# Reordering the front of a fused mLSTM and mixture-of-experts kernel: where statistics, square roots, queries and copies stand in each engine's queue

## The chip, the core and the metric

The kernel runs on one core of one Trainium2 chip. The metric is the device time of one execution in microseconds (us). All of the work is fp32 except for a few bf16 helper matrices.

## What is computed

The input is x, 16 sequences of 256 tokens with 128 features. It is normalised per token, an mLSTM attention and a top-1 mixture of experts both read the normalised xn, and the result is `x + s * silu(ffn)`:

```python
x = L0_attn_x                                  # 16 x 256 x 128
xn = _layernorm(x, axis=-1)
s = _L0_attn_ref(xn, wq, wk, wv, wi, bi, wf, bf, ln_w)
g = _silu(_L0_ffn_ref(xn, router_w, router_b, w1, b1, w2, b2))
x = x + s * g

# _L0_attn_ref, 4 heads of 32: q, k, v are 4x4 block-diagonal maps of xn
gate_in = jnp.concatenate([x, x, x], axis=-1)
ig = (gate_in @ wi.T + bi); fg = (gate_in @ wf.T + bf)
log_fg = jax.nn.log_sigmoid(fg)                # cumulated over the sequence: cs
log_D = where(tril, cs_i - cs_j, -inf) + ig_j
max_log_D = jnp.max(log_D, axis=-1, keepdims=True)
C = (q @ k.T / sqrt(dh)) * jnp.exp(log_D - max_log_D)
normaliser = jnp.maximum(abs(sum(C)), jnp.exp(-max_log_D))
h = C / (normaliser + eps) @ v                 # then a layernorm per head, times (1 + ln_w)

# _L0_ffn_ref, 8 experts: the expert with the largest router logit computes
a, g = jnp.split(x @ w1[i] + b1[i], 2, axis=-1)
y = (a * sigmoid(g)) @ w2[i] + b2[i]
```

## The kernel before

Nothing schedules this kernel: each engine has one program written out by hand, and semaphores join them. An engine goes through its queue in the written order, so an instruction that waits holds all that stand behind it on that engine. Engines: TensorE (PE), VectorE (DVE), ScalarE (ACT), GpSimd (POOL), and SyncE (SP), which issues most DMAs.

**Front.** The 32 tiles of 128 tokens form four groups of eight, g = 0 to 3. VectorE computes mean and variance of a group in `variance(g)` (`bn_stats` L696, `bn_aggr` L699, then `veps` L701, which raises `s_var`). ScalarE takes the square root in `rsqrt_start(g)` (L483, waits for `s_var` at g + 1, raises `s_y0`). VectorE turns it into 1/sqrt by a reciprocal and one Newton step in `newton(g)` (L707 to L711, waits for `s_y0`, raises `s_rsq`). In `normalised(g)` the eight tiles are then normalised, shared by VectorE (L716), ScalarE (L488) and GpSimd (L399). TensorE transposes them four at a time (`transposes(q)`, q = 0 to 7, L1037), ScalarE copies each four to SBUF (`xT_copy(q)`, L493), and TensorE multiplies them with the value, router and gate weights (`values(q)`, L1052), whose results `evac_vl(c)`, c = 0 to 10, takes out of PSUM: on VectorE for c = 1, 3, 5, 7, 9 (L723), on ScalarE for the others (L499). The small weights are first combined on TensorE (L1062 to L1065; their block matrices come from GpSimd, L392) and copied by ScalarE (L508 to L510). `keep_warm(n, b)` (L1028) issues n matmuls on zeros.

**Gates, routing, queries.** After `values(7)`: bias, log-sigmoid and running sums of the gates on VectorE, ScalarE and TensorE (L1092 to L1096), a running maximum, three-part bf16 splits, and the selection matmuls `pick` (L1109), of which `pick_copy` makes `sel`; `right_rows`, `left_rows` and two VectorE operations (L810, L812) prepare the operands of the decay exponents. `queries(c)`, c = 0 to 7 (L1082), computes the queries of 512 tokens, `evac_q(c)` copies them (L535). Router counting (L1116 to L1118) gives `rank`, six small VectorE operations (L819 to L824) give each expert's start, `positions()` each token's place, `experts_of_blocks()` each block's expert. `fl_row`, the exponential of the negated maximum, is transposed into `tm`, which the final normalisation of the attention (L924) reads.

**Attention loop.** For each of the B = 16 sequences: scores (L1159), decay exponents on TensorE (L1148, L1149) and their exponentials on ScalarE (`decay`, L586), the product on VectorE (`weigh`, L859), `values_sum` (L1169), `evac_u` (L593) and `token_rows` (L1180), and `outputs` (L864). Sequence b + 1's scores wait for sequence b's `weigh`. VectorE also subtracts w1's last row from its other rows within the loop (`fold_half`, L898), and GpSimd scatters the 32 tiles to their experts' blocks by indirect DMA (L443).

**Experts.** 39 blocks of 128 tokens: `rowsT` (L1131), `hidden` (L1195), `down` (L1204), and a final part that adds all up. TensorE works nearly without a gap here.

## Time and profile before

| | |
|---|---|
| time, median of 3 runs | 240.93 us (239.75 to 241.77) |
| profiled execution, its own time | 240.99 us |
| its span, first to last instruction | 239.2 us |
| busy: PE / PE weight loads | 209.1 us (87%) / 170.8 us (71%) |
| busy: DVE / ACT / POOL | 181.8 us (76%) / 136.5 us (57%) / 100.0 us (42%) |
| chain that ended last, by engine | PE 67%, DVE 11%, issue 6%, ACT 5%, DMA 5% |

Busy shares are means over stages that have different limits. The profile's chain of waits follows the end of the program back from instruction to instruction, and says which engine's work stood in the way at each moment. The profiled execution lies 0.06 us from the median, so that sums can be made against it.

### The profile page before, as it was taken

Reading aid. Unit: us, or ns where it says so; the run is one execution under the profiler, and the core shown is the slowest. Engines: PE = TensorE matmul, PEld = TensorE weight load, DVE = VectorE, ACT = ScalarE, POOL = GpSimd, SP = SyncE. Lnnn points to the kernel's source line nnn. Section 1 sums busy time; section 2 is a strip of 40 time slices with the busy share of each in tenths; the row PEclk is TensorE's granted clock in tenths of the full one; section 3 lists DMA queues with packets and bytes.
Section 4 is the critical chain, followed back from the end, with each engine's and each line's share of the span. In section 5 each row is a group of like instructions: output and inputs, shape, how many; then the busy total and the mean of one; then the engine's idle time right before and its main releaser. Section 6 shows DMA issues by size and latency. Waiting matters only on the chain.

```text
span 239.2 us, 6066 instructions
## 1 busy us (share of the span) xinstructions
PE 209.1 (87%) x1824; PEld 170.8 (71%) x1832; DVE 181.8 (76%) x505; ACT 136.5 (57%) x313; POOL 100.0 (42%) x128
## 2 busy tenths in 40 slices
PE   0688879689999999979999999999999999999650
PEld 0568744335555555559999999999999999986310
DVE  6997378299989986648777988898889789671490
ACT  0276756779788796754555555555555655540110
POOL 7553200027777776000333364425533464366150
PEclk9988999999999999999999999999999999999975
DMA  6999999501441111401097021102101000000994
GB/s 175 266 419 418 282 299 394 221 3 46 146 137 53 49 53 59 115 21 33 15 261 204 26 58 52 55 22 62 44 30 50 28 25 25 26 11 13 251 315 137
DMA packets 29730, 29.30 MB, mean 122 GB/s; under 512 B 3295, under 2 KB 24807, under 8 KB 29697
## 3 DMA queue, kind: packets, MB, share of 16 engines
q1 hardware_dynamic: 26258, 24.59, 33.0%
q0 software_dynamic: 2272, 4.22, 5.4%
q8 instruction: 16, 0.26, 0.5%
q10 hardware_dynamic: 1168, 0.10, 0.4%
q14 instruction: 16, 0.13, 0.2%
HBM read 20.01 MB, written 9.34 MB: 123 GB/s over the span
## 4 chain that ended last, share of the span: by engine, by line
PE 67%; DVE 11%; issue 6%; ACT 5%; DMA 5%; DVEq 1%; SPq 1%; POOL 1%; ACTq 0%; POOLq 0%
PE bank L1195 13%; PE head_bank L1195 13%; PE bank L1204 12%; PE head_bank L1159 5%; PE bank L1169 5%; PE bank L1149 4%; PE head_bank L1052 4%; PE bank L1180 3%; PE bank L1148 3%; DMA xw<-y_tokens 2%; DVE stats L696 2%; PE bank L1037 2%; PE bank L1082 2%; DVE cm L859 2%; PE head_bank L1131 1%
## 5 line engine op out<-in xcount | busy, mean ns | idle before, releaser
L449 POOL DMA_INDIRECT y_tokens<-ffn,idx x39 | 39.2, 1004 | 76.3 <-DVE ffn L992 74.0
L443 POOL DMA_INDIRECT xs_sorted<-xw,pos x32 | 33.0, 1031 | 36.3 <-DVE pos L831 26.9
L1204 PE MATMUL bank<-w_sb,dm 128*128 x312 | 41.3, 275 | 0.5 <-DVE dm L976 0.5
L1195 PE MATMUL bank<-xsT,wc 128*128 128x128 f32 x320 | 39.3, 276 | 0.1
L1204 PEld LDWEIGHTS bank<-w_sb,dm 128*128 128x128 f32 x312 | 38.0, 192 | 0.7 <-issue 0.7
L1195 PEld LDWEIGHTS bank<-xsT,wc 128*128 128x128 f32 x320 | 37.4, 192 | 0.5 <-DVE wc L851 0.3
L1195 PE MATMUL head_bank<-xsT,wc 128*128 128x128 f32 x304 | 37.0, 275 | 0.0
L1195 PEld LDWEIGHTS head_bank<-xsT,wc 128*128 128x128 f32 x304 | 35.4, 192 | 0.0
L859 DVE TENSOR_TENSOR cm<-dm,head_bank 128x1024 f32<-128x1024 f32 (+1 forms) x32 | 29.0, 948 | 6.3 <-ACT dm L586 3.5
L600 ACT ACTIVATE wc<-w_sb 128x512 f32 x39 | 24.6, 630 | 14.3 <-issue 14.3
L586 ACT ACTIVATE dm<-bank 128x512 f32<-128x512 f32 x48 | 26.9, 594 | 4.5 <-PE bank L1149 3.5
L606 ACT ACTIVATE xsT<-head_bank 127x128 f32<-127x128 f32 x38 | 10.5, 277 | 27.8 <-PE head_bank L1131 27.8
L851 DVE COPY wc<-w_sb 128x512 f32 x39 | 16.6, 425 | 10.3 <-issue 9.0
L1149 PE MATMUL bank<-right,left 128*128 128x512 bf16 x48 | 15.7, 379 | 2.6 <-ACT x_sb L535 1.0
L1159 PEld LDWEIGHTS head_bank<-x_sb,xnT 32*128 32x128 f32 x256 | 11.7, 184 | 8.0 <-issue 7.7
L976 DVE TENSOR_TENSOR dm<-bank,dm 128x512 f32<-128x512 f32 x20 | 13.6, 681 | 3.7 <-ACT dm L612 2.0
L1159 PE MATMUL head_bank<-x_sb,xnT 32*128 32x256 f32 (+1 forms) x256 | 15.0, 347 | 0.5 <-DVE cm L859 0.4
L976 DVE TENSOR_TENSOR dm<-head_bank,dm 128x512 f32<-128x512 f32 x19 | 13.0, 684 | 2.3 <-ACT dm L612 2.3
L984 DVE TENSOR_TENSOR ffn<-bank,b_sb 128x128 f32<-128x128 f32 x39 | 11.2, 287 | 4.4 <-PE bank L1204 2.1
L656 ACT ACTIVATE ffn<-ffn 128x128 f32<-128x128 f32 x39 | 11.8, 302 | 4.9 <-DVE ffn L984 4.9
L1169 PE MATMUL bank<-cm,u_all 128*32 128x256 f32 (+1 forms) x256 | 13.7, 332 | 0.0
L612 ACT ACTIVATE dm<-bank 128x512 f32<-128x512 f32 x20 | 11.6, 581 | 2.9 <-PE bank L1195 2.9
(199 smaller groups left out, 352.0 us busy)
## 6 DMA issues: line engine op xcount, KB each, us to landing
x_sb<-in_L_attn_x SPq DMA_DIRECT2D x16, 256.0 KB, 5.1
w_sb<-in_L_ffn_w SPq DMA_DIRECT2D x8, 512.0 KB, 8.2
wc<-in_L_ffn_w SPq DMA_DIRECT2D x5, 512.0 KB, 17.1
xs_sb<-xs_sorted SPq DMA_DIRECT2D x13, 193.5 KB, 2.8
xs_sorted<-b_sb SPq DMA_DIRECT2D x1, 2048.0 KB, 17.3
xw<-y_tokens SPq DMA_DIRECT2D x8, 256.0 KB, 4.6
out_x<-xw SPq DMA_DIRECT2D x8, 256.0 KB, 3.6
y_tokens<-ffn,idx POOLq DMA_INDIRECT x39, 2.3
```

Of the source, the lines that this page charges most:

```text
L443: pool.indirect_dma_start(xs_dram, bass.IndirectOffsetOnAxis(ap=pos[:, t:t + 1], axis=0), xw[:, t, :], None).then_inc(s_scat, 16)
L449: pool.indirect_dma_start(y_dram, bass.IndirectOffsetOnAxis(ap=idx[:, j:j + 1], axis=0), ys_sb[:, j // CH % 2, j % CH, :], None, bounds_ch ...
L586: act.activation(dm[:, b % 2, :, m, :], bank[(3 * b + m) % 2][:, :].rearrange("p (h t) -> p h t", h=NH), ACT.Exp).then_inc(s_dm, 1)
L600: act.activation(wc[:, j % 3, HID:H2], w1_sb[:, bass.ds(e, 1), HID:H2], ACT.Copy).then_inc(s_wc, 1)
L851: dve.tensor_copy(wc[:, j % 3, 0:HID], w1_sb[:, bass.ds(e, 1), 0:HID]).then_inc(s_wv, 1)
L859: dve.tensor_tensor(cm[:, b % 2, :, m0:m1, :], dm[:, b % 2, :, m0:m1, :], head_bank[:, :, m0 * P:m1 * P].rearrange("p h (m t) -> p h m t", ...
L976: dve.tensor_tensor(uT[:, j % 2, :, :].rearrange(flat), bank[2 * (j % 2)][:, :], sg[:, j % 2, :, :].rearrange(flat), ALU.mult).then_inc(s_ ...
L1149: pe.matmul(bank[n % 2][:, :], left[:, b % 4, s0:s0 + P], right[:, :, j, t0:t0 + P], start=(m == 1), stop=True).then_inc(s_ld, 1)
L1159: last = pe.matmul(head_bank[:, h, 2 * k * P:(2 + k) * P], xnT[hs, b * S + k * P:b * S + (k + 1) * P], q_all[hs, b * S + k * P:(b + 1) * S ...
L1169: last = pe.matmul(bank[6][h * DH:(h + 1) * DH, k * P:S], u_all[:, 2 * b + k, h, 0:DH], cm[:, b % 2, h, 2 * k:2 + k, :].rearrange("p m t - ...
L1195: last = pe.matmul(bank[2 * (j % 2) + k][:, c * P:(c + 1) * P], wc[:, j % 3, m:m + P], xsT[:, j % 2, :], start=True, stop=True)
L1204: last = pe.matmul(bank[6 + j % 2][:, 0:D], uT[:, j % 2, c, :], w2_sb[:, bass.ds(e * (HC * D) + c * D, D)], start=(c == 0), stop=(c == HC ...
```

## The change

On TensorE, twelve warming matmuls instead of four, ahead of the wait for the small weights instead of behind it; queries 2 and 3 move ahead of the gate sums; query 7 goes behind the first scores; the transposes of `fl_row` move into the attention loop (sequence 3).

On ScalarE, the table of the square root is loaded by an explicit instruction ahead of the first root instead of by a dummy root behind four more DMA issues; these four issues go behind root 0; root 1 goes behind `normalised(0)`. The copies of queries 6 and 7, of `rank`, and `left_rows(1)` are done by VectorE. The sigmoid table is loaded one sequence later, and the first two weight copies are made one sequence earlier.

On VectorE, the Newton step of each group stands between the first half and the second half of the next group's statistics (g = 0, 1), `variance(3)` stands behind `normalised(2)` instead of ahead of `evac_vl(1)`, and the experts of blocks are spread over nine sequences, one operation in each. Of the eight tiles of a group, VectorE normalises two instead of three, GpSimd three instead of two.

Core of the diff (declarations, memory views and the waits for `tm` are left out, as are the lines of places shown as order rows below):

```diff
@@ gpsimd
             def normalised(g):
                 pool.wait_ge(s_rsq, g + 1)
-                for t in range(GS * g + 3, GS * (g + 1), 4):
+                for t in (GS * g + 3, GS * g + 6, GS * g + 7):
@@ scalar
-                for t in (GS * g + 1, GS * g + 5, GS * g + 6):
+                for t in (GS * g + 1, GS * g + 2, GS * g + 5):
...
-            act.wait_ge(s_zero, 1)
-            act.activation(spare[:, 0:1], zeros[:, 0:1], ACT.Sqrt).then_inc(s_dummy, 1)
+            act.preload_act_table_set("sqrt_and_others")
             rsqrt_start(0)
-            rsqrt_start(1)
...
             normalised(0)
+            rsqrt_start(1)
             xT_copy(0)
             rsqrt_start(2)
...
-            evac_q(0)
-            evac_q(1)
+            for c in range(4):
+                evac_q(c)
...
+            def forget_row():
+                act.wait_ge(s_fd, 1)
+                act.activation(fdiff, fdiff, ACT.Exp).then_inc(s_flr, 1)
...
-                if b + 2 == B - 1:
+                if b == 1:
+                    forget_row()
+                if b == B - 2:
                     act.preload_act_table_set("sigmoid_and_others")
...
-                if b == B - 3:
+                if b == B - 4:
...
                     copy_w(0)
-                if b == B - 2:
+                if b == B - 3:
                     copy_w(1)
@@ vector
-                for t in (GS * g, GS * g + 2, GS * g + 4):
+                for t in (GS * g, GS * g + 4):
...
+            link(stats_of(0, 0, GS))
             variance(0)
-            variance(1)
+            stats_of(1, 0, GS // 2)
             newton(0)
             normalised(0)
-            variance(2)
+            link(stats_of(1, GS // 2, GS))
+            variance(1)
+            stats_of(2, 0, GS // 2)
             newton(1)
             normalised(1)
+            link(stats_of(2, GS // 2, GS))
+            variance(2)
+            evac_vl(1)
+            newton(2)
+            normalised(2)
+            link(stats_of(3, 0, GS))
+            variance(3)
+            evac_vl(3)
...
-            variance(3)
-            evac_vl(1)
-            newton(2)
-            normalised(2)
-            evac_vl(3)
...
+            dve.wait_ge(s_cnt, 1)
+            dve.tensor_copy(rank[:, :], bank[4][:, 0:E * T + E + 1]).then_inc(s_rank, 1)
+            dve.tensor_scalar(left[:, 1, :], sel[:, 0, :], lmask[:, 0, 1:2], lmask[:, 1, 1:2], ALU.mult, ALU.add).then_inc(s_lf1, 1)
+
+            def evac_q(c):
+                dve.wait_ge(s_q, c + 1)
+                dve.tensor_copy(q_all[:, c * 512:(c + 1) * 512], xT_bank[c % 4][:, :]).then_inc(s_qed, 1)
+
+            evac_q(NQA)
...
                     weigh(b)
+                    if b == 0:
+                        evac_q(NQA + 1)
                     if b >= 1:
                         outputs(b - 1)
-                    if b == 0:
-                        positions()
-                    if 1 <= b < 4:
-                        for _ in range(3):
-                            step_of = next(blocks, None)
-                            if step_of is not None:
-                                link(step_of)
+                    if b < 2:
+                        for place in itertools.islice(places, 2):
+                            link(place)
+                    if 2 <= b < 11:
+                        step_of = next(blocks, None)
+                        if step_of is not None:
+                            link(step_of)
@@ tensor
             pe.wait_ge(s_zero, 1)
+            keep_warm(12, 7)
             pe.wait_ge(s_wsmall, 16 * 6)
             pe.wait_ge(s_const, 9)
-            keep_warm(4, 7)
```

On VectorE, from the statistics of group 3 (before) to the normalisation of group 2, the queue reads before:

```order
L696 BN_STATS stats<-x_sb 128x6 x8
L699 BN_AGGR mv<-stats 128x2 x8
L701 TENSOR_SCALAR veps<-mv 128x8
L723 COPY cm<-head_bank 128x48
L724 COPY u_all<-head_bank 128x12x31
L707 RECIPROCAL ry<-ra 128x8
L708 TENSOR_TENSOR rb_<-ry 128x8
L709 SCALAR_TENSOR_TENSOR ry<-rb_,veps 128x8
L710 SCALAR_TENSOR_TENSOR rstd<-ry 128x8
L711 SCALAR_TENSOR_TENSOR nmr<-mv,rstd 128x8
L716 TENSOR_SCALAR xw<-x_sb,rstd,nmr 128x128 x3
```

The same stretch of VectorE's queue in the changed kernel, where L728 and L729 are `evac_vl(1)`, L712 to L716 `newton(2)`, L721 `normalised(2)`, and the last three rows the statistics of group 3:

```order
L728 COPY cm<-head_bank 128x48
L729 COPY u_all<-head_bank 128x12x31
L712 RECIPROCAL ry<-ra 128x8
L713 TENSOR_TENSOR rb_<-ry 128x8
L714 SCALAR_TENSOR_TENSOR ry<-rb_,veps 128x8
L715 SCALAR_TENSOR_TENSOR rstd<-ry 128x8
L716 SCALAR_TENSOR_TENSOR nmr<-mv,rstd 128x8
L721 TENSOR_SCALAR xw<-x_sb,rstd,nmr 128x128 x2
L698 BN_STATS stats<-x_sb 128x6 x8
L704 BN_AGGR mv<-stats 128x2 x8
L706 TENSOR_SCALAR veps<-mv 128x8
```

The statistics of group 3, which ended ahead of the copy `evac_vl(1)` and of the group-2 Newton step, now come behind both and behind the normalisation of group 2.

On ScalarE, from the copies of the combined weights to the pair `xT_copy(2)`, `xT_copy(3)`, before (`ra` is a root, `xw` a normalised tile, `xnT` an `xT_copy`, `cm` and `u_all` are `evac_vl(0)`):

```order
L508 ACTIVATE wvl<-head_bank 128x128
L509 ACTIVATE wvl<-head_bank 128x8
L510 ACTIVATE wqk<-head_bank 128x128
L488 ACTIVATE xw<-x_sb,nmr,rstd 128x128 x3
L493 ACTIVATE xnT<-bank 128x512
L483 ACTIVATE ra<-veps 128x8
L493 ACTIVATE xnT<-bank 128x512
L488 ACTIVATE xw<-x_sb,nmr,rstd 128x128 x3
L499 ACTIVATE cm<-head_bank 128x48
L500 ACTIVATE u_all<-head_bank 128x12x31
L483 ACTIVATE ra<-veps 128x8
L493 ACTIVATE xnT<-bank 128x512 x2
```

ScalarE's queue in the changed kernel, from the same copy of the weights:

```order
L512 ACTIVATE wvl<-head_bank 128x128
L513 ACTIVATE wvl<-head_bank 128x8
L514 ACTIVATE wqk<-head_bank 128x128
L491 ACTIVATE xw<-x_sb,nmr,rstd 128x128 x3
L486 ACTIVATE ra<-veps 128x8
L496 ACTIVATE xnT<-bank 128x512
L486 ACTIVATE ra<-veps 128x8
L496 ACTIVATE xnT<-bank 128x512
L491 ACTIVATE xw<-x_sb,nmr,rstd 128x128 x3
L502 ACTIVATE cm<-head_bank 128x48
L503 ACTIVATE u_all<-head_bank 128x12x31
L486 ACTIVATE ra<-veps 128x8
```

Root 1 now stands behind `normalised(0)`; the places of roots 2 and 3, ahead of `xT_copy(1)` and of `xT_copy(2)`, are unchanged.

On TensorE, from the query behind the selection matmuls to the first decay exponents and scores, before (L1082 a query, L1116 to L1118 the router's counts, L1122 the transposes of `fl_row`, L1159 the scores):

```order
L1082 MATMUL bank<-xnT,wqk 128x512
L1116 MATMUL head_bank<-oh,tril 128x256
L1117 MATMUL head_bank<-ohc,ones_bf 128x256
L1118 MATMUL head_bank<-ohc,ones_bf 128x9
L1122 MATMUL head_bank<-ident,cm 128x64 x2
L1082 MATMUL bank<-xnT,wqk 128x512
L1148 MATMUL bank<-maskn,ident_bf 128x512
L1149 MATMUL bank<-right,left 128x512 x2
L1082 MATMUL bank<-xnT,wqk 128x512
L1159 MATMUL head_bank<-x_sb,xnT 128x256 x4
L1159 MATMUL head_bank<-x_sb,xnT 128x128 x4
```

The same place in the changed kernel (L1106 a query, L1166 and L1167 decay exponents, L1180 the scores):

```order
L1106 MATMUL bank<-xnT,wqk 128x512
L1139 MATMUL head_bank<-oh,tril 128x256
L1140 MATMUL head_bank<-ohc,ones_bf 128x256
L1141 MATMUL head_bank<-ohc,ones_bf 128x9
L1166 MATMUL bank<-maskn,ident_bf 128x512
L1167 MATMUL bank<-right,left 128x512 x2
L1180 MATMUL head_bank<-x_sb,xnT 128x256 x4
L1180 MATMUL head_bank<-x_sb,xnT 128x128 x4
L1166 MATMUL bank<-maskn,ident_bf 128x512
L1167 MATMUL bank<-right,left 128x512
L1106 MATMUL bank<-xnT,wqk 128x512
```

Two transposes and one query have left the stretch ahead of the first scores, and the last query stands behind them.

## Rows read from the trace of the kernel before

**Rows 1.** Windows: stretch, length, busy us and count of each engine, PEclk, DMA.

```profile
16.00:17.00 1.00, 1.00 (x6) 1.00 (x5) 1.00 (x6) 1.00 (x4) 0.48 (x4) 0.50 1.05 430
```

**Rows 2.** Source line L1028, warming matmuls: durations min/median/max in ns, first and last start.

```profile
L1028 PE MATMUL head_bank<-zeros x18: 379/379/379, 219.3 to 223.0; 128*128 128x256 f32 x18
L1028 PE MATMUL bank<-zeros x8: 634/634/767, 7.8 to 10.9; 128*128 128x256 f32 x8
```

**Rows 3.** Timeline: start, duration, instruction, idle before; to the first normalised tiles.

```profile
0.79 0.31 POOL L362 MEMSET zeros<- 128x256 f32 x1 [0.29 <-POOLq L1278]
7.80 1.12 POOL L392 TENSOR_TENSOR dm<-block,nat 128x128 f32<-128x128 f32 x3 [2.58 <-DMA nat<-in_L_attn_wk]
13.23 0.28 ACT L508 ACTIVATE wvl<-head_bank 128x128 f32<-128x128 f32 x1 [3.96 <-PE head_bank L1065]
13.62 1.26 ACT L488 ACTIVATE xw<-x_sb,nmr,rstd 128x128 f32<-128x128 f32 x3
```

**Rows 4.** Timeline, VectorE, ScalarE and GpSimd from the statistics of group 3.

```profile
15.92 1.63 DVE L696 BATCH_NORM_STATS2 stats<-x_sb 128x6 f32<-128x128 f32 x8
18.26 0.17 DVE L701 TENSOR_SCALAR veps<-mv 128x8 f32<-128x8 f32 x1
18.46 0.21 ACT L483 ACTIVATE ra<-veps 128x8 f32<-128x8 f32 x1 [0.55 <-DVE veps L701]
18.66 0.60 ACT L493 ACTIVATE xnT<-bank 128x512 f32<-128x512 f32 x1
19.48 0.21 DVE L723 COPY cm<-head_bank 128x48 f32<-128x48 f32 x1 [1.05 <-PE head_bank L1052]
20.06 0.19 DVE L707 RECIPROCAL ry<-ra 128x8 f32<-128x8 f32 x1
21.09 0.91 DVE L716 TENSOR_SCALAR xw<-x_sb,rstd,nmr 128x128 f32<-128x128 f32 x3
21.16 1.00 POOL L399 TENSOR_SCALAR xw<-x_sb,rstd,nmr 128x128 f32<-128x128 f32 x2 [4.68 <-DVE nmr L711]
```

**Rows 5.** Timeline, TensorE: transposes and values.

```profile
15.62 2.14 PE L1052 MATMUL head_bank<-wvl,xnT 128*128 128x144 f32 x8
17.56 1.06 PE L1037 MATMUL bank<-ident,xw 128*128 128x128 f32 x4
22.42 1.15 PE L1052 MATMUL head_bank<-wvl,xnT 128*128 128x144 f32 x8
29.31 1.25 PE L1052 MATMUL head_bank<-wvl,xnT 128*128 128x144 f32 x8 [0.92 <-ACT xnT L493]
```

**Rows 6.** Timeline: from the selection matmuls to the second scores.

```profile
38.81 1.47 PE L1109 MATMUL head_bank<-cm,dm 128*128 128x256 bf16 x12
43.32 0.17 DVE L819 SCALAR_TENSOR_TENSOR ecount_i<-rank 128x8 int32<-128x8 f32 x1 [0.22 <-ACT rank L576]
44.79 0.59 PE L1149 MATMUL bank<-right,left 128*128 128x512 bf16 x2 [0.97 <-ACT x_sb L535]
46.17 0.94 PE L1159 MATMUL head_bank<-x_sb,xnT 32*128 32x256 f32 x16
50.36 0.94 PE L1159 MATMUL head_bank<-x_sb,xnT 32*128 32x256 f32 x16
```

**Rows 7.** Timeline, VectorE and GpSimd in the attention loop.

```profile
53.69 0.47 DVE L834 TENSOR_TENSOR bcmp<-blk_start,eend 128x312 f32<-128x312 f32 x1
66.06 1.82 DVE L859 TENSOR_TENSOR cm<-dm,head_bank 128x1024 f32<-128x1024 f32 x2 [0.47 <-PE head_bank L1159]
87.52 1.81 DVE L859 TENSOR_TENSOR cm<-dm,head_bank 128x1024 f32<-128x1024 f32 x2
93.83 0.96 POOL L443 DMA_INDIRECT xs_sorted<-xw,pos  x1 [0.30 <-issue]
```

**Rows 8.** Timeline: the end of the loop.

```profile
101.11 1.28 ACT L630 ACT_TABLE_LOAD   x1
104.10 2.02 PE L1195 MATMUL bank<-xsT,wc 128*128 128x128 f32 x16
```

More of the change, by code:

```diff
@@ L1 @@
+import itertools
 from contextlib import ExitStack
@@ L688, in rsqrt_steps, with stats_of @@
                 return y
-            def variance(g):
-                gt = slice(GS * g, GS * (g + 1))
-                for t in range(GS * g, GS * (g + 1)):
+            def stats_of(g, t0, t1):
+                for t in range(GS * g + t0, GS * g + t1):
                     if t % TG == 0:
@@ L696, in variance @@
                     last = dve.bn_stats(stats[:, t, :], x_sb[:, t, :])
-                link(last)
+                return last
+            def variance(g):
+                gt = slice(GS * g, GS * (g + 1))
                 for t in range(GS * g, GS * (g + 1)):
@@ L782, in _ @@
             link(next(router))
+            link(next(router))
             dve.wait_ge(s_gg, 1)
@@ L1082, in queries @@
                 pe.matmul(xT_bank[c % 4][:, :], wqk[:, :], xnT[:, c * 512:(c + 1) * 512], start=True, stop=True).then_inc(s_q, 1)
-            queries(0)
-            queries(1)
+            for c in range(4):
+                queries(c)
             pe.wait_ge(s_tri, 2)
@@ L1112, in _ @@
                     last.then_inc(s_picked, 1)
-            queries(5)
+            queries(6)
             pe.wait_ge(s_oh, 1)
@@ L1118, in _ @@
             pe.matmul(bank[4][:, E * T:E * T + E + 1], ones_bf[:, :], ohc[:, 0:E * T + 1:T], start=True, stop=True).then_inc(s_cnt, 1)
-            pe.wait_ge(s_flr, 1)
-            pe.wait_ge(s_grest, 1)
-            for k in range(2):
-                last = pe.transpose(bank[5][:, k * R:(k + 1) * R], fl_row[:, k * P:(k + 1) * P], ident[R:P, R:P])
-            last.then_inc(s_flp, 1)
-            queries(6)
             def rowsT(j):
```

94 lines of the change are left out of this document (52 added, 42 removed).

## The prediction

> **What bounds the kernel now.** I read the page first, for the engines' shares and the chain that ended last: 67% of it is TensorE, and from the first expert block at 104.10 us on it is TensorE with hardly a gap [rows 8]. The change touches nothing behind that point. So the question is only when this block starts, and the whole time moves by as much. Then I read the chain in order of time and the timeline ahead of 104 us. There the bound changes hands: VectorE's statistics and TensorE at its low clock until 20 us, a ping-pong of ScalarE and TensorE until `values(7)` starts at 29.31 [rows 5], a chain of small steps until the second scores at 50.36 [rows 6], then the attention loop. In each stretch the reader is to see what the engine at the head of the chain waits for, and what stands in front of it in its queue. I cost the change stretch by stretch against the profiled 240.99 us, which is the median of the runs, 240.93, for all that matters here.
>
> **Warming first (a gain of 2.6 us on the small weights).** In before the warming starts when the weights have landed, at 7.8. A matmul on zeros shows two passes; eight passes start 0.44 us apart ((10.9 - 7.8)/7), eighteen late in the kernel 0.22 us apart ((223.0 - 219.3)/17) [rows 2]. These are the two levels of the clock, 1.2 and 2.4 GHz. Twelve matmuls are 24 passes, and they start when the zeros are written, at 1.1 (0.79 + 0.31) [rows 3]. If half of them run at the low level, they end at 1.1 + 12 x 0.44 + 12 x 0.22 = 9.0, just when GpSimd's three blocks are there (7.80 + 1.12 = 8.9) [rows 3]. From the last warming pass to ScalarE's first weight copy it took 13.23 - 11.3 = 1.9 us at the low level; so the copy comes at 10.9 at the latest, I take 10.6. The gain is 2.6 us. Bounds: none at all, if all 24 passes are slow (1.1 + 10.6 + 1.9 = 13.6), and 3.1.
>
> **Root 1, Newton 1, root 2 (the gain is spent).** ScalarE now takes root 1 behind `normalised(0)`. Its three tiles start 0.39 after the weight copy and take 1.26 [rows 3], the root 0.2, so VectorE's Newton step 1 starts near 12.5; it had half a group's statistics to do meanwhile, and waits about 1 us. Then, in VectorE's new order: Newton 1.03 (21.09 - 20.06), two tiles 0.6 (two thirds of 0.91), half of group 2's statistics and its variance 1.5 (18.26 - 15.92 = 2.34 less half of 1.63), and 0.2 to root 2 [rows 4]: 15.9. ScalarE has nothing to do from about 13, because `xT_copy(1)` and `normalised(1)` stand behind root 2. With 0.2, a copy of 0.6, two tiles at 0.42 and a hand-over of 0.1, `transposes(2)` starts at 17.6; it started at 17.56 before [rows 5]. TensorE idles about 3 us ahead of it. In before an idle stretch of 1 us was followed by a granted clock of 0.50 in 16 to 17 us [rows 1], so I count this place at 1.2 GHz again, as before: `evac_vl(1)` at 17.6 + 1.9 = 19.5, where it was (19.48) [rows 4].
>
> **The hold at root 3 (a loss of 5.8 us).** This is the term that decides. Before, VectorE finished group 3's variance at 18.26, ahead of `evac_vl(1)`; root 3 went at 18.46 and `xT_copy(2)` at 18.66 [rows 4]. Now the variance of group 3 stands behind `evac_vl(1)`, Newton 2 and `normalised(2)`, while ScalarE still has root 3 ahead of `xT_copy(2)` and `xT_copy(3)`. So from 19.5: 0.58 to Newton (20.06 - 19.48), 1.03, 0.6, statistics and variance 2.34, 0.2, 0.2 = 4.95. `xT_copy(2)` starts at 24.5 instead of 18.66. Queued behind root 3 on ScalarE is all of its remaining share of the front; TensorE waits for it with `values(2)`, and VectorE then with `evac_vl(3)`. Bounds: 4.5 (weights at 10.1, and TensorE at 2.4 GHz, where values take 1.15 against 2.14 [rows 5]) and 5.9.
>
> **From `xT_copy(2)` to `values(7)` (a loss of 1.2 us more).** This took 29.31 - 18.66 = 10.65 us, and the queues are the same. What is ready early (Newton 2, VectorE's and GpSimd's tiles) takes little off, since ScalarE's own tiles and copies alternate with TensorE. But TensorE has idled over 4 us and comes back at 1.2 GHz. Two groups of values cost 0.99 more each (2.14 - 1.15), the transposes between them some 0.4; part of it is hidden behind ScalarE's tiles. I take 1.2 between 0 and 2.4. `values(7)` starts 7.0 us late, at 36.3.
>
> **From `values(7)` to the second scores (a gain of 4.45 us).** All times here are those of before, without the shift. The gate sums need the logarithms, which are there 4.6 us after `values(7)` starts; four queries at two passes of 0.43 fit into that gap, so moving two of them ahead costs nothing at 2.4 GHz, and 3.4 us at 1.2 GHz. The selection matmuls at 38.81 were held by queries until about 38.7 and come 0.2 earlier. They take 1.47 [rows 6], then query 6 0.9 and the counts 0.3, so `rank` can be copied at 41.3. Then VectorE, which is the bound here: `rank` 0.4, `left` 0.3, the copy of query 6, six small operations at 0.2 (0.17 and a gap [rows 6]), `weigh(0)` 1.82 [rows 7]. A VectorE copy of 512 columns from PSUM has no row. ScalarE takes 0.60 for it [rows 4], and the loop's `weigh`, three times as many columns, 1.82, a third of which is 0.61; with a fixed part of its own I take 0.7, with bounds of 0.6 and 0.8. That gives 45.7, and the second scores at 45.9 instead of 50.36: 4.45, bounds 4.0 and 4.6. Decay exponents (44.79 to 41.4) and first scores (46.17 to 41.9) gain less in need than in time; they are off the path.
>
> **The attention loop (a loss of 0.6 us).** Query 7's copy lies beside TensorE's period of 3.5 us. The steps of the expert blocks, four of about 0.47 [rows 7] and four of 0.2, leave sequences 1 to 3, where they made the period longer by 0.7 in sum; `forget_row` costs ScalarE 0.4 in sequence 1. But from sequence 5 to 9 they come on top of two folds each. There six periods of `weigh` took 87.52 - 66.06 = 21.46 us [rows 7], about 1.2 of it idle; 1.7 more work leaves 0.5 to 1.3. In sum +0.6, bounds 0 and 1.3. At the loop's end the sigmoid table (1.28, at 101.11 [rows 8]) moves behind `evac_u(14)`; the first weight copies leave, but ScalarE must still load it between that copy and the first block: +0.1. GpSimd's last scatter (93.83 [rows 7]) starts only 1.1 us earlier relative to the shift, while the first block comes 3.9 earlier; with over 7 us between them I count nothing, at most 0.9.
>
> **Sum.** 240.99 + 5.8 + 1.2 - 4.45 + 0.6 + 0.1 = **244.2 us**. The third tile of GpSimd (0.5 each) ends before ScalarE's third and costs nothing while that holds.
>
> GpSimd's two tiles took 1.00 us while VectorE worked on its own three in 0.91 [rows 4]; neither shows a halt. The Trainium skill ("SBUF — State Buffer", Who interferes with whom) says that a VectorE `tensor_scalar` in a two-port mode and a GpSimd instruction exclude each other for a whole instruction. By that rule a third GpSimd tile could hold VectorE's statistics by about 0.5 in each of three groups, and the sum would be 245.7; the trace does not bear it out, and I give it 1 in 20.
>
> **Rivals.** (1) *The hold without the slow clock.* TensorE comes back at 2.4 GHz, the delay at `values(7)` is 4.7, and the loop absorbs the expert steps: 240.99 + 4.7 - 4.45 + 0.1 = 241.3. For it: the values at 22.42 ran at the high level although TensorE had waited for `transposes(4)` just before [rows 5]. Against it: an idle stretch of 1 us was enough to be followed by 0.50 [rows 1]. Chance 0.2. (2) *The backlog is caught up, faster.* Behind the hold nothing but queued work is left: ScalarE has six copies of 0.5, six tiles of 0.42 and four `evac_vl` of 0.6, 8 us in sum, TensorE about 8 at 2.4 GHz. If the two run side by side instead of alternating, `values(7)` comes 8.1 behind `xT_copy(2)`, not 10.65. With the hold at its least, 4.5 - 2.55 - 4.45 gives 238.5. It decides for faster once the hold and what follows cost under 2 us. Against it: each copy feeds the next matmul in turn. Chance 0.12. (3) *The warming stays slow*, weights at 13.6 and everything above moves by 2.8: 247.0. Chance 0.1. The port rule has 0.05, the forecast 0.53.
>
> **Range and chances.** The forecast's own bounds are 240.99 + 4.5 - 4.6 and 240.99 + 5.9 + 2.4 - 4.0 + 1.3 + 0.9, so 240.9 to 247.5, its ends unlikely together. With rival 1 inside and half of rivals 2 and 3 outside, 240.2 to 246.6 holds 8 in 10. A change of 1% (2.4 us) is about what this kernel's runs can tell. Faster by more is rival 2: 0.12. Within 1%, 238.5 to 243.3, are rival 1 and the forecast's lower tail: 0.33. Slower is the rest: 0.55.
>
> **What would show it.** ScalarE idle about 5 us ahead of a root that waits for VectorE's `veps`, right ahead of two `xT_copy`; before it, a shorter idle at root 2; TensorE idle beside it, then values of about 2.1 us; `values(7)` near 36; second scores about 16.6 us behind it instead of 21.05; the expert blocks as before. The prediction is wrong if group 3's variance is ready when ScalarE asks for root 3, if the clock does not fall, or if `values(7)` follows the hold in much less than 10 us.

## The result, and the profile after

The changed kernel takes **244.0 us** (median of 4 runs, 243.42 to 245.26) against 240.8 for the kernel before, measured beside it (4 runs, 239.75 to 241.77). The ratio is 1.0141, with a 95% interval of 1.0079 to 1.0203: slower. The forecast was 244.2, and 240.2 to 246.6. The profiled execution took 243.42 us, the least of the four; its span is 241.7 against 239.2.

Two rows of the profile's page after (40 slices of 6.04 us, in tenths) show where to look. TensorE's granted clock is down in the third to fifth slice, and ScalarE's busy share falls to 0 in the fourth (18.1 to 24.2 us):

```profile
ACT  2340776679879698764655555665555656541020
PEclk9957799999999999999999999999999999999975
```

The hold itself, in ScalarE's timeline of the changed kernel (columns: start, duration, engine, line, operation, tile, count, and in brackets the idle time before it and what ended it):

```profile
11.70 0.21 ACT L486 ACTIVATE ra<-veps 128x8 f32<-128x8 f32 x1
12.65 0.60 ACT L496 ACTIVATE xnT<-bank 128x512 f32<-128x512 f32 x1 [0.74 <-PE bank L1061]
15.39 0.21 ACT L486 ACTIVATE ra<-veps 128x8 f32<-128x8 f32 x1 [2.15 <-DVE veps L706]
...
23.76 0.21 ACT L486 ACTIVATE ra<-veps 128x8 f32<-128x8 f32 x1 [6.06 <-DVE veps L706]
23.88 1.06 ACT L496 ACTIVATE xnT<-bank 128x512 f32<-128x512 f32 x2
```

ScalarE sits idle 6.06 us ahead of root 3, and two copies that TensorE needs go 0.1 us behind it. What VectorE does meanwhile, in its timeline:

```profile
19.04 0.21 DVE L728 COPY cm<-head_bank 128x48 f32<-128x48 f32 x1 [3.68 <-PE head_bank L1076]
...
19.61 0.19 DVE L712 RECIPROCAL ry<-ra 128x8 f32<-128x8 f32 x1
...
21.21 1.63 DVE L698 BATCH_NORM_STATS2 stats<-x_sb 128x6 f32<-128x128 f32 x8
22.88 0.64 DVE L704 BATCH_NORM_AGGREGATE mv<-stats 128x2 f32<-128x6 f32 x8
23.56 0.17 DVE L706 TENSOR_SCALAR veps<-mv 128x8 f32<-128x8 f32 x1
```

VectorE is idle 3.68 us ahead of `evac_vl(1)`, at the very time in which the kernel before ran group 3's statistics [rows 4]; now they start at 21.21. TensorE's timeline shows the other end of it (values are L1076, transposes L1061):

```profile
24.51 2.13 PE L1076 MATMUL head_bank<-wvl,xnT 128*128 128x144 f32 x8 [3.70 <-ACT xnT L496]
26.67 1.09 PE L1061 MATMUL bank<-ident,xw 128*128 128x128 f32 x4
27.55 1.43 PE L1076 MATMUL head_bank<-wvl,xnT 128*128 128x144 f32 x8
...
35.11 1.25 PE L1076 MATMUL head_bank<-wvl,xnT 128*128 128x144 f32 x8 [0.92 <-ACT xnT L496]
...
51.52 0.39 PE L1166 MATMUL bank<-maskn,ident_bf 128*128 128x512 bf16 x1 [0.47 <-ACT dm L587]
51.74 0.38 PE L1167 MATMUL bank<-right,left 128*128 128x512 bf16 x1
52.05 0.94 PE L1180 MATMUL head_bank<-x_sb,xnT 32*128 32x256 f32 x16
...
61.51 0.38 PE L1166 MATMUL bank<-maskn,ident_bf 128*128 128x512 bf16 x1 [0.68 <-ACT right L569]
...
106.64 1.58 PE L1224 MATMUL bank<-xsT,wc 128*128 128x128 f32 x12 [0.92 <-issue]
```

`values(7)` starts at 35.11 (29.31 before [rows 5]), the second scores at 52.05 (50.36 [rows 6]), the first expert block at 106.64 (104.10 [rows 8]). So 5.80 us are lost up to `values(7)`, 4.11 come back up to the second scores (16.94 against 21.05), and 0.85 are lost again in the loop and at its end: +2.54, which is the span's +2.5.

### The profile page after: what moved, and what is told of

It is laid out like the page before. It is cut to its first block, busy times and chain, and to the rows that moved or that the text cites. A ratio compares the mean times of both kernels' runs of the same rounds, so it can differ in the third digit from the quotient of the medians.

```text
span 241.7 us, 6116 instructions
## 1 busy us (share of the span) xinstructions
PE 216.7 (90%) x1848; PEld 176.5 (73%) x1848; DVE 182.5 (76%) x505; ACT 134.7 (56%) x308; POOL 101.2 (42%) x132
## 3 DMA queue, kind: packets, MB, share of 16 engines
q0 software_dynamic: 2272, 4.22, 5.4%
## 4 chain that ended last, share of the span: by engine, by line
PE 63%; DVE 11%; issue 9%; DMA 5%; ACT 3%; DVEq 2%; POOL 1%; SPq 1%; ACTq 1%; POOLq 0%
PE bank L1224 11%; PE head_bank L1224 11%; PE bank L1233 10%; PE head_bank L1180 5%; PE head_bank L1076 4%; PE bank L1192 4%; PE bank L1166 4%; PE bank L1167 4%; PE bank L1209 3%; PE bank L1061 2%; DMA xw<-y_tokens 2%; DMA nat<-in_L_attn_wk 2%; PE bank L1106 2%; DVE cm L877 1%; PE head_bank L1147 1%
## 5 line engine op out<-in xcount | busy, mean ns | idle before, releaser
L449 POOL DMA_INDIRECT xs_sorted<-xw,pos x32 | 32.5, 1017 | 36.0 <-DVE pos L849 26.6
L587 ACT ACTIVATE dm<-bank 128x512 f32<-128x512 f32 x48 | 26.9, 595 | 5.7 <-PE bank L1167 4.6
L1180 PEld LDWEIGHTS head_bank<-x_sb,xnT 32*128 32x128 f32 x256 | 11.7, 184 | 7.4 <-issue 6.7
L1076 PE MATMUL head_bank<-wvl,xnT 128*128 128x144 f32 x64 | 12.7, 358 | 4.6 <-ACT xnT L496 4.6
L1167 PE MATMUL bank<-right,left 128*128 128x512 bf16 x48 | 15.6, 379 | 0.0
L1076 PEld LDWEIGHTS head_bank<-wvl,xnT 128*128 128x128 f32 x64 | 11.3, 248 | 5.8 <-ACT xnT L496 5.5
L1180 PE MATMUL head_bank<-x_sb,xnT 32*128 32x256 f32 (+1 forms) x256 | 15.0, 347 | 0.2 <-DVE cm L877 0.2
L1008 DVE TENSOR_TENSOR ffn<-bank,b_sb 128x128 f32<-128x128 f32 x39 | 11.2, 288 | 3.6 <-PE bank L1233 1.4
```

The source lines that it names most:

```text
L449: pool.indirect_dma_start(xs_dram, bass.IndirectOffsetOnAxis(ap=pos[:, t:t + 1], axis=0), xw[:, t, :], None).then_inc(s_scat, 16)
L587: act.activation(dm[:, b % 2, :, m, :], bank[(3 * b + m) % 2][:, :].rearrange("p (h t) -> p h t", h=NH), ACT.Exp).then_inc(s_dm, 1)
L1076: last = pe.matmul(bank[2 + c % 4][:, t % 3 * VL:(t % 3 + 1) * VL], xnT[:, t * P:(t + 1) * P], wvl[:, :], start=True, stop=True)
L1167: pe.matmul(bank[n % 2][:, :], left[:, b % 4, s0:s0 + P], right[:, :, j, t0:t0 + P], start=(m == 1), stop=True).then_inc(s_ld, 1)
L1180: last = pe.matmul(head_bank[:, h, 2 * k * P:(2 + k) * P], xnT[hs, b * S + k * P:b * S + (k + 1) * P], q_all[hs, b * S + k * P:(b + 1) * S ...
```

## The experiments

Each time is a median. The kernel before took 240.84 (13 runs, 240.11 to 242.49) beside e1 to e4, and 240.80 (17 runs, 239.66 to 242.49) beside e5 to e8, on another chip. The marks below are start times in us of the profiled executions: ScalarE's first weight copy, `xT_copy(2)`, `values(7)`, the second scores, the first expert block. The gaps between marks are what I compare, because the small weights land up to 1.4 us apart in executions of the same front (GpSimd's first block on them started between 7.42 and 8.82), and all later marks move with them.

| kernel | weights | `xT_copy(2)` | `values(7)` | scores 1 | experts | time, us |
|---|---|---|---|---|---|---|
| before | 13.23 | 18.66 | 29.31 | 50.36 | 104.10 | 240.8 |
| changed | 10.16 | 23.88 | 35.11 | 52.05 | 106.64 | 244.0 |
| e1, root 3 ready | 11.56 | 19.48 | 31.93 | 48.86 | 103.45 | 238.5 |
| e2, late variance alone | 13.23 | 24.55 | 35.74 | 56.79 | 110.53 | 246.3 |
| e3, old VectorE front | 10.42 | 18.48 | 29.62 | 46.56 | 101.15 | 237.8 |
| e4, warming alone | 10.23 | 18.62 | 28.42 | 50.94 | 104.67 | 241.5 |
| e5, busy in the hold | 10.98 | 25.52 | 35.89 | 52.83 | 107.41 | 244.2 |
| e6, dip filled | 10.37 | 18.68 | 28.28 | 49.34 | 103.07 | 240.2 |
| e7, fills later | 11.31 | 18.10 | 28.46 | 45.40 | 99.99 | 237.0 |
| e8, sums before queries | 10.91 | 18.17 | 28.54 | 46.40 | 100.98 | 238.5 |

### e1: the changed kernel with group 3's variance ahead

```diff
@@ vector
             variance(2)
+            link(stats_of(3, 0, GS))
+            variance(3)
             evac_vl(1)
             newton(2)
             normalised(2)
-            link(stats_of(3, 0, GS))
-            variance(3)
```

> The changed kernel with one step moved back: the statistics and the variance of group 3 stand again ahead of evac_vl(1) and Newton 2 on VectorE. Theory (the hold at root 3 is the price): ScalarE has root 3 by about 18 us, xT_copy(2) near 18.1, values(7) near 28.9 instead of 35.1, and the rest as in the changed kernel: 237.8 us (236.5 to 239), faster than before by 1.2%. Rival (the slow clock and root 2 are the price, the hold is hidden): values(7) not earlier than 33 us, 242 to 244 us.

238.51 us (237.41 to 240.34, 4 runs), ratio to before 0.989 (0.9842 to 0.9937). ScalarE's root 3 has no wait ahead of it:

```profile
19.23 0.21 ACT L486 ACTIVATE ra<-veps 128x8 f32<-128x8 f32 x1
```

`xT_copy(2)` starts at 19.48. Two moved lines turn the slower kernel into a faster one: the hold, with the slow clock behind it, cost 5.5 us by the medians. By the marks it is 4.6 (20.37 us from the first weight copy to `values(7)` instead of 24.95). `values(7)` at 31.93 missed the expected 28.9: the weights came 1.4 later in this execution, and with the hold gone `xT_copy(3)` waited 2.17 for `transposes(3)`, which TensorE did at a granted clock of 0.50.

### e2: only that, in the kernel before

```diff
@@ vector
-            variance(3)
             evac_vl(1)
             newton(2)
             normalised(2)
+            variance(3)
```

> The kernel before with one step moved: variance(3) behind normalised(2) on VectorE, nothing else. Theory (hold): xT_copy(2) near 24.5 instead of 18.66, values(7) 5.5 to 7 us late, 246.5 to 248 us in all (246.9), slower than before by 2.5%. Rival (the hold costs only in company of the other edits, since the backlog is caught up): within 2 us of before.

246.29 us (245.59 to 247.46, 4 runs), ratio 1.0218 (1.0175 to 1.0261): +5.5. ScalarE waits as in the changed kernel:

```profile
24.43 0.21 ACT L483 ACTIVATE ra<-veps 128x8 f32<-128x8 f32 x1 [6.58 <-DVE veps L701]
```

In the profiled execution, the slowest of the four, `xT_copy(2)` moved by 5.89, `values(7)` by 6.43, the expert blocks by 6.43. Added or taken away, the order of one variance has one price, and nothing behind it absorbs any of it. Rival 2 falls: with the backlog queued, `values(7)` still came 11.2 us behind `xT_copy(2)`, not 8.1.

### e3: the changed kernel with before's whole order of VectorE's statistics

```diff
@@ vector (the front; the rest of the change stays)
-            stats_of(1, 0, GS // 2)
+            link(stats_of(1, 0, GS))
+            variance(1)
             newton(0)
             normalised(0)
...
             newton(1)
             normalised(1)
...
+            link(stats_of(3, 0, GS))
+            variance(3)
             evac_vl(1)
```

> The changed kernel with the whole order of statistics and Newton steps of the kernel before on VectorE; warming first, early table and the whole tail stay. Theory: without the wait at root 2, normalised(1) on ScalarE starts near 14.1 instead of 16.0, and without the hold xT_copy(2) near 17; values(7) near 27 us, 235.5 us in all (234.5 to 237), faster than before by 2.2% and than the kernel with root 3 alone put right by 2 us. Rival (root 2 costs nothing, because TensorE at 1.2 GHz or the copies set the pace anyway): as that kernel, 237.8.

237.83 us (236.9 to 238.33, 4 runs), ratio 0.9869 (0.9828 to 0.9911). The expected 235.5 was missed: the median is 0.7 below e1's, and the intervals of the two overlap widely. The tiles of group 1 came at 15.24, not 14.1. VectorE's timeline has the reason:

```profile
12.49 0.64 DVE L704 BATCH_NORM_AGGREGATE mv<-stats 128x2 f32<-128x6 f32 x8
13.17 1.21 DVE L706 TENSOR_SCALAR veps<-mv 128x8 f32<-128x8 f32 x1
13.25 1.13 DVE L712 RECIPROCAL ry<-ra 128x8 f32<-128x8 f32 x1
14.44 0.17 DVE L713 TENSOR_TENSOR rb_<-ry 128x8 f32<-128x8 f32 x1
```

Two operations of 0.17 and 0.2 us take 1.21 and 1.13, and both end at 14.38. In GpSimd's timeline of the same kernel a run of casts and fills without a gap ends there, at 14.35:

```profile
11.65 1.46 POOL L414 CAST dm<-ident 128x64 bf16<-128x64 f32 x6
13.04 0.34 POOL L415 MEMSET u_all<- 128x128 f32 x1
...
14.13 0.22 POOL L419 MEMSET ones_bf<- 128x128 bf16 x1
```

The kernel before has a smaller case of it (0.55 for `veps` at 13.15, while its fills end at 13.67). e7 and e10 test this.

### e4 and e6: the warming alone, and a pause filled

e4 is the kernel before with twelve warming matmuls first; e6 adds to it four passes on zeros at two places:

```diff
@@ tensor (e4, against the kernel before)
             pe.wait_ge(s_zero, 1)
+            keep_warm(12, 7)
             pe.wait_ge(s_wsmall, 16 * 6)
             pe.wait_ge(s_const, 9)
-            keep_warm(4, 7)
@@ tensor (e6, against e4)
+            pe.wait_ge(s_qe, 4)
+            keep_warm(2, 7)
             pe.wait_ge(s_flr, 1)
...
             queries(6)
+            keep_warm(2, 7)
```

> The kernel before with the twelve warming matmuls ahead of the waits, nothing else. Theory: weights ready near 10.2 instead of 13.2, normalised(1) on ScalarE limited by Newton 1 (14.5) instead of 16.1, values(7) 1.0 to 1.5 us earlier: 239.7 us (239 to 240.3), which three rounds can hardly tell from before, so the trace decides. Rival (the early weights buy nothing, root order gives it back): values(7) within 0.3 us of 29.3.

> The kernel before with the warming alone (241.48), and two more matmuls on zeros (four passes each) at two places where TensorE pauses: behind the counts (about 41.6) and behind query 6 (about 42.9). In the run with the warming alone values(7) came 0.9 us earlier and the clock stood at 0.50 from 43.8 to 47. If this clock ate the gain, it now stays at 1.00 there, the first scores come 1.4 us earlier (45.3 to 45.5) and the time is 240.1 to 240.4. If the gain was lost to something else (an order of copies on ScalarE, the transfers), the first scores stay near 46.7 and the time at 241.5, or above it by what the passes cost.

e4: 241.48 us (239.94 to 242.59, 10 runs), ratio 1.001 (0.9979 to 1.0042). The 3.0 us on the weights became 0.9 at `values(7)`, a little less than expected, since VectorE's statistics set the pace there (root 3 waited 2.18 us for `veps`), and nothing that can be told in the time. The windows of e4 show where the 0.9 went (columns: stretch, its length, busy time of PE, PEld, DVE, ACT, POOL, granted clock, DMA share, GB/s):

```profile
43.00:44.00 1.00, 0.32 (x1) 0.14 (x2) 0.51 (x3) 0.86 (x2) 0.00 (x0) 0.79 0.65 229
44.00:45.00 1.00, 1.00 (x4) 0.56 (x3) 0.00 (x0) 0.00 (x0) 0.00 (x0) 0.50 1.00 377
45.00:46.00 1.00, 1.00 (x3) 0.25 (x1) 0.00 (x0) 0.00 (x0) 0.00 (x0) 0.50 0.52 191
46.00:47.00 1.00, 1.00 (x5) 0.24 (x8) 0.00 (x0) 0.14 (x1) 0.00 (x0) 0.51 0.18 74
```

In this execution TensorE paused 1.06 and 0.76 us, and came back at 1.2 GHz in front of query 7, which ScalarE's exponentials and VectorE wait for; `values(7)` to the first scores took 18.34 us instead of 16.86. The kernel before had the same pauses 0.9 us later and kept 1.00 (its trace reads 0.97 for the second, but the record of one decay exponent is missing in it), and so did e2, with 1.06 and 0.76. So the length of these pauses alone doesn't decide it, and one trace of each kernel doesn't tell how often e4 has the dip. In e6, with TensorE busy, the same stretch reads 1.00:

```profile
43.00:44.00 1.00, 0.89 (x6) 0.47 (x6) 0.41 (x3) 0.73 (x2) 0.00 (x0) 1.00 0.70 256
44.00:45.00 1.00, 1.00 (x4) 0.36 (x2) 0.00 (x0) 0.00 (x0) 0.00 (x0) 1.00 0.79 240
45.00:46.00 1.00, 1.00 (x17) 0.72 (x16) 0.00 (x0) 0.74 (x2) 0.00 (x0) 1.00 0.96 328
```

e6 takes 240.20 us (12 runs, 239.64 to 241.7), 1.3 below e4 by the medians and 0.8 by the two ratios, whose intervals just overlap. The distance to the first scores is 16.87 again: in the profiled execution of e4 the dip had eaten the gain. Against the kernel before e6 is 0.9978 (0.9953 to 1.0003): the warming, alone and protected, is worth 0.6 us by the medians, which isn't clear of noise, and 1.03 by the mark of the first expert block.

### e5: TensorE kept busy in the hold

```diff
@@ tensor (changed kernel, behind transposes(3))
+                if q == 3:
+                    keep_warm(5, 5)
```

> The changed kernel, and five more matmuls on zeros (ten passes) behind transposes(3), while TensorE waits for xT_copy(2). If the 1.2 GHz behind the hold comes from TensorE's idle time there, values(2) at about 24.5 takes 1.15 us instead of 2.13 and values(7) starts at 34.2 to 34.5 instead of 35.11: 243.2. If ScalarE's copies set the pace there, or if the clock falls all the same, values(7) stays at 35.1: 244.0.

244.19 us (243.0 to 245.46, 4 runs): by the time, nothing. By the trace, the clock theory holds all the same. TensorE's timeline:

```profile
26.16 1.25 PE L1076 MATMUL head_bank<-wvl,xnT 128*128 128x144 f32 x8 [0.52 <-ACT xnT L496]
```

`values(2)` took 1.25 instead of 2.13, and from `xT_copy(2)` to `values(7)` it was 10.37 us instead of 11.23. This 0.86 was lost ahead of it in the same execution, where root 2 came 6.06 us behind the first weight copy instead of 5.23, and the weights themselves were 0.82 late. VectorE's timeline has the place:

```profile
9.90 0.64 DVE L704 BATCH_NORM_AGGREGATE mv<-stats 128x2 f32<-128x6 f32 x8
10.57 2.73 DVE L706 TENSOR_SCALAR veps<-mv 128x8 f32<-128x8 f32 x1
```

An operation of 0.17 us took 2.73 and ended at 13.30. GpSimd's timeline of this kernel:

```profile
10.61 1.43 POOL L414 CAST dm<-ident 128x64 bf16<-128x64 f32 x6
11.98 0.33 POOL L415 MEMSET u_all<- 128x128 f32 x1
...
13.07 0.21 POOL L419 MEMSET ones_bf<- 128x128 bf16 x1
```

The run of eleven instructions ends at 13.28. In the changed kernel's own profiled execution the same `veps` started at 10.94, in the middle of the casts, and took 0.25, and in e1 it took 0.26. So this hold can be part of the change's cost in some executions and not in others. How often, three traces with this order don't tell.

### e7: the fills behind GpSimd's tiles of group 1

```diff
@@ gpsimd (e3, the five memsets)
-            pool.memset(u_all[:, :, :, DH - 1:DH], 1.0).then_inc(s_uones, 1)
...
-            pool.memset(ones_bf[:, :], 1.0).then_inc(s_cnt0, 1)
             normalised(1)
+            pool.memset(u_all[:, :, :, DH - 1:DH], 1.0).then_inc(s_uones, 1)
...
+            pool.memset(ones_bf[:, :], 1.0).then_inc(s_cnt0, 1)
```

> The changed kernel with the old order of VectorE's statistics (237.83), and GpSimd's five constant fills of 13.04 to 14.35 us moved behind its tiles of group 1. In that run two VectorE operations of 0.17 us on 8 elements a row (veps at 13.17, the reciprocal at 13.25) ended at 14.38, just behind the last fill. If the fills held them, they take 0.17 and 0.19 now, root 2 and the tiles of group 1 come 1.0 us earlier (13.4 and 14.2), and the time is 236.8. If they waited for something else, nothing moves before the tiles of group 1, and the time is 237.8; if the fills now hold other VectorE work between 15.6 and 17 us, veps of group 3 ends later than 18.3 and the gain is gone again.

237.03 us (236.39 to 237.59, 4 runs), ratio 0.9841 (0.9799 to 0.9884): below both kernels, and the lowest median of e1 to e8; it is 0.8 below e3's, though the two intervals overlap, so the trace has to carry the reading. In VectorE's timeline:

```profile
13.58 0.17 DVE L706 TENSOR_SCALAR veps<-mv 128x8 f32<-128x8 f32 x1
13.66 0.20 DVE L712 RECIPROCAL ry<-ra 128x8 f32<-128x8 f32 x1
...
17.61 0.34 DVE L706 TENSOR_SCALAR veps<-mv 128x8 f32<-128x8 f32 x1
```

From the start of that `veps` to ScalarE's tiles of group 1 it takes 1.12 us instead of 2.07 (from the weight copy 3.39 instead of 4.82, but the weights were 0.9 later here and VectorE hardly waits for them). This repeats: with the fills in their old place `veps` took 1.19 to 1.21 in all four traces of this order (e3, e8, e9, e10), and with the fills moved 0.17 in all three (e7, e11, e12). In e7 `veps` of group 3, now beside GpSimd instructions, takes 0.34 instead of 0.17. The statistics themselves (1.63 for eight) are the same beside the fills as without.

### e8: two queries behind the gate sums again

```diff
@@ tensor (e3; ScalarE's copies in the same order)
-            for c in range(4):
-                queries(c)
+            queries(0)
+            queries(1)
             pe.wait_ge(s_tri, 2)
...
-            queries(4)
-            queries(5)
+            for c in range(2, 6):
+                queries(c)
```

> The changed kernel with the old order of VectorE's statistics (237.83), and two of the four queries ahead of the gate sums put behind them again, with their copies on ScalarE. By my account the sums start no earlier (they wait for the logarithms, at 4.65 us behind values(7)), but the selection matmuls, which VectorE holds until 39.06 in that run, now wait for four queries, 3.6 us behind the sums: 39.9, so 0.85 later, and the second scores with them: 238.7. If VectorE's and ScalarE's own work behind it sets the pace and the queries are free on both sides, the time stays within 0.2 of 237.8; if the four queries ahead cost the sums something, it is below 237.6.

238.47 us (237.81 to 239.35, 4 runs), +0.64. The sums start 4.63 us behind `values(7)`, as in e3 (4.65): four queries ahead of them are free. The selection matmuls come 0.91 later, and the second scores 0.92 (17.86 us behind `values(7)` instead of 16.94).

### e9 to e12: another chip

These four ran on a chip on which the kernel before took 254.05 us (7 runs, 253.44 to 255.85). In all four profiled executions one period of the attention loop, from about 59 us on, took 12 to 15 us instead of 3.5 to 4.2; in e11 TensorE sat idle 8.62 and ScalarE 10.00 us in it. What caused it the traces don't show, and it hides differences of 1 us in the times. Ratios to the kernel before there: e9 0.985 (0.9771 to 0.9929), e10 0.9846 (0.9784 to 0.9908), e11 0.9852 (0.9772 to 0.9932); for e12, whose runs lie 5 us apart, there is none (252.15, 247.44 to 252.53). Up to 52 us the traces are undisturbed, and I read only those.

e9 puts query 7 back to where the kernel before had it:

```diff
@@ scalar (e3)
             pick_copy(2, 2)
+            evac_q(7)
@@ tensor
             log_decay(0, 1)
+            queries(7)
...
             log_decay(0, 2)
-            queries(7)
```

> The changed kernel with the old order of VectorE's statistics (237.83), and query 7 issued and copied as in the kernel before: behind the first two decay exponents on TensorE, by ScalarE ahead of its first exponentials. In the kernel before VectorE sat idle 3.48 us ahead of weigh(0) until ScalarE's exponentials came, which stood behind this copy. If that queue holds the larger part of the gain, ScalarE's first exponential starts at 44.1 instead of 42.47 (query 7 ends on TensorE at 43.5, its copy takes 0.6), weigh(0) and the second scores come 1.4 to 1.7 later, and the time is 239.3. If VectorE's own steps set the pace (it has one copy of 512 columns less), the second scores move by less than 0.3 and the time is 237.6 to 238.1.

ScalarE's timeline of e9:

```profile
42.59 0.60 ACT L540 ACTIVATE x_sb<-bank 128x512 f32<-128x512 f32 x1 [1.37 <-PE bank L1103]
43.09 1.08 ACT L588 ACTIVATE dm<-bank 128x512 f32<-128x512 f32 x2
```

The first exponentials start 14.41 us behind `values(7)` instead of 12.85 in e3, and VectorE waits 1.21 for them ahead of `weigh(0)`. The second scores come 17.86 behind instead of 16.94: +0.92, a smaller step than expected, in the expected direction.

e10 issues the five fills of e3 twice, with one wait of GpSimd for the first five between them:

```diff
@@ gpsimd (e3)
+            pool.memset(u_all[:, :, :, DH - 1:DH], 1.0).then_inc(s_twice, 1)
...
+            pool.memset(ones_bf[:, :], 1.0).then_inc(s_twice, 1)
+            pool.wait_ge(s_twice, 5)
             pool.memset(u_all[:, :, :, DH - 1:DH], 1.0).then_inc(s_uones, 1)
```

> The changed kernel with the old order of VectorE's statistics (237.83), with GpSimd's five fills issued twice, 1.3 us more work on GpSimd ahead of its tiles of group 1. If a run of GpSimd instructions holds VectorE's small operations to its end, veps of group 2 and the reciprocal of group 1 end 1.3 us later (near 15.7), and the time is 239.1. If VectorE gets in where GpSimd waits once for its own first fills, they end near 14.4 as before; GpSimd's tiles of group 1 then come 0.6 to 1.3 late, behind ScalarE's, and the time is 238.0 to 238.8. If there is no such hold, only that second effect is left.

In VectorE's timeline `veps` ends where GpSimd waited once:

```profile
12.92 1.21 DVE L713 TENSOR_SCALAR veps<-mv 128x8 f32<-128x8 f32 x1
13.00 1.13 DVE L719 RECIPROCAL ry<-ra 128x8 f32<-128x8 f32 x1
14.19 0.17 DVE L720 TENSOR_TENSOR rb_<-ry 128x8 f32<-128x8 f32 x1
```

GpSimd's first five fills end at 14.11 and the second five run from 14.16 to 15.54:

```profile
13.90 0.21 POOL L420 MEMSET ones_bf<- 128x128 bf16 x1
14.16 0.33 POOL L422 MEMSET u_all<- 128x128 f32 x1
```

So here one wait of GpSimd ended the hold. VectorE's operations behind it then ran at their usual 0.17, and its two tiles in 0.62, beside the second five fills: a run of GpSimd instructions doesn't hold everything that meets it, and which operation is held the runs don't settle.

e11 is e7 with the copy of `rank` on ScalarE; e12 is e11 with `forget_row` behind the right and left rows of sequence 1:

```diff
@@ scalar (e11)
             pick_copy(2, 2)
+            act.wait_ge(s_cnt, 1)
+            act.activation(rank[:, :], bank[4][:, 0:E * T + E + 1], ACT.Copy).then_inc(s_rank, 1)
@@ scalar (e12, in the loop)
-                if b == 1:
-                    forget_row()
...
                 if b + 4 < B:
                     left_rows(b + 4)
+                if b == 1:
+                    forget_row()
```

> The version with the fills moved (237.03), with the copy of the counts (rank, 0.43 us on VectorE) on ScalarE behind its second copy of the gate rows. ScalarE has 0.3 us of slack there, VectorE none up to weigh(0): weigh(0) and the second scores come 0.3 to 0.4 earlier, 236.7. If ScalarE's exponentials are as late as VectorE's chain, the shift costs what it gives: 237.0 to 237.1.

> As the run before (rank on ScalarE), and the exponential of the forget row on ScalarE put behind the right and left rows of sequence 1. In the changed kernel TensorE waited 0.68 us for a right row ahead of the scores of sequence 4, and that period was 0.23 longer than before. If the forget row caused it, the period of 4.22 falls to 4.0 and the time is 0.2 to 0.25 below the run before it: 236.5. If the wait only moves to the next period (the copy of its transposes in sequence 3), nothing changes.

In e11 `weigh(0)` starts 14.08 us behind `values(7)` (14.46 in e3), but the second scores 16.94 behind, exactly as before. In TensorE's timeline of e11:

```profile
44.49 0.39 PE L1164 MATMUL bank<-maskn,ident_bf 128*128 128x512 bf16 x1 [0.47 <-ACT dm L589]
44.72 0.38 PE L1165 MATMUL bank<-right,left 128*128 128x512 bf16 x1
45.03 0.94 PE L1178 MATMUL head_bank<-x_sb,xnT 32*128 32x256 f32 x16
```

The same wait stands in the changed kernel at 51.52: a decay exponent ahead of the second scores waits 0.47 for ScalarE's exponential, not for VectorE, whose `weigh(0)` ended at 51.38, 0.67 ahead of them (VectorE's timeline of the changed kernel):

```profile
49.56 1.82 DVE L877 TENSOR_TENSOR cm<-dm,head_bank 128x1024 f32<-128x1024 f32 x2
```

The profile's chain of the changed kernel goes the same way: right rows on ScalarE (46.09), decay exponents and first scores on TensorE, query 7 itself (0.86), one exponential (0.61), and the second scores. Neither `rank` nor query 6 is on it. For e12, the wait of 0.68 us for the right row is gone (2.41 us from the scores of sequence 3 to the next exponent in e11, 1.83 in e12), but whether the period gets shorter lies in the disturbed stretch (in all four traces TensorE pauses 1 us or more from about 56 us on, ahead of the long period): open.

## Why the prediction was right

**Weights.** Forecast 10.6, measured 10.16; 24 passes took from 1.15 to 8.10. With before's order of VectorE too the gain is spent before group 2, since the statistics bind: `xT_copy(2)` starts at 18.62 in e4 against 18.66.

**Root 2, `transposes(2)`, `evac_vl(1)`.** Forecast 15.9, 17.6, 19.5; measured 15.39, 16.95, 19.04. All near half a microsecond early, as the weights were. TensorE's clock was lower than "as before": 0.50 from 12 to 21 us instead of 16 to 19. Up to `transposes(2)` this cost nothing, because root 2 came later still.

**The hold.** Forecast 5.8, measured 5.2 (23.88 against 18.66), by the mechanism and in the order given; e1 and e2 price it, together with the slow clock behind it, at 5.5 us by the medians, from both sides, and at 4.6 and 6.4 by the marks up to `values(7)`. The forecast for the two was 7.0, the change of the mark 5.8.

**From `xT_copy(2)` to `values(7)`.** Forecast +1.2, measured +0.58 (11.23 against 10.65). The mechanism was right, the size half: only one group of values ran wholly at 1.2 GHz, since the clock was back at 28. With TensorE kept busy (e5, one trace) it was 10.37. Rival 1, the hold without the slow clock, didn't come.

**`values(7)` to the second scores.** Forecast 4.45, measured 4.11. The sum was near, but one step named the wrong engine. It said "VectorE, which is the bound here"; e11 took 0.4 us off VectorE, `weigh(0)` came earlier, and the second scores didn't. What binds at the end is TensorE's decay exponents and ScalarE's exponentials in turn. VectorE's own sum was good: it ended 16.27 us behind `values(7)`, forecast 16.4. The second scores came 0.67 behind it instead of the 0.2 allowed, so the number was near only because the two chains end so close together. What the gain is made of: with query 7 back in its old place 0.92 of it goes (e9), with four queries behind the sums instead of two another 0.92 (e8, one query more than the kernel before had there). The rest, over 2 us, is the other work taken from ScalarE and out of the chain (`left_rows(1)`, `rank`, the copy of query 6, `forget_row` with its transposes); it wasn't taken apart.

**The loop and its end.** Forecast +0.6 and +0.1, measured +0.70 (scores 1 to 15 take 50.73 against 50.03) and +0.15. The places are partly others: a large step is the period from sequence 3 to 4, 4.22 against 3.99, with TensorE waiting 0.68 for a right row that stands behind `forget_row`. The sequences 1 to 3 gave back only 0.17, not 0.7.

**The port rule** had 1 in 20 and one argument, that the tiles of 1.00 and 0.91 showed no halt. For the tiles this held: GpSimd's three took 1.37 and VectorE's two 0.66 side by side. But the trace of the kernel before held a halt elsewhere, `veps` at 0.55 against a median of 0.17, and I didn't read it. e5, e3 and e7 show holds of 2.6, 1.0 and, with the fills moved, none. The Trainium skill ("SBUF — State Buffer", Who interferes with whom) says that in a two-port mode whoever issues first has the shared pair for the whole instruction; the traces agree that a VectorE `tensor_scalar` can be blocked fully, and show one blocked over a run of GpSimd instructions, eleven in e5, not over one. They don't show it each time: 0.25 for the `veps` of the changed kernel that started amid the same casts. In the same execution three operations of Newton 0 took 0.33, 0.32 and 0.32 instead of 0.17 beside GpSimd's three products (7.42 to 8.53), so there VectorE got in between. The plainest sign stood in the expert part of the kernel before, where TensorE sets the pace: three VectorE operations on 128x32 elements took 2.68, 2.35 and 2.35 us, each to the end of one GpSimd product of 2.39 to 2.40 (timelines of VectorE and GpSimd):

```profile
141.54 2.68 DVE L930 TENSOR_SCALAR veps<-ssum 128x32 f32<-128x32 f32 x1
141.77 2.39 POOL L457 TENSOR_TENSOR u_all<-cm,gamma 128x1024 f32<-128x1024 f32 x1
```

**Sum.** +5.2, +0.6, -4.1, +0.7, +0.15 make 2.55; the span moved by 2.5 and the median by 3.2. The forecast was 3.2: the hold and the slow clock were put 1.2 too dear, the gain 0.35 too high and the loop 0.15 too cheap. That it meets the median to 0.2 us is partly luck: these errors cancel in part, and the profiled execution, the least of the four, lies 0.6 below the median for a reason that its trace can't show.
